# Query and key/value projections of a transformer layer as seven half-width products per pair of heads, with weights summed in place and a new first and last stretch

## Chip, core and metric

The kernel runs on one core of a Trainium2 chip. The metric is the device time of one execution in microseconds (us). The core has a matrix engine (TensorE, PE in the profile, its weight loads PEld), a vector engine (VectorE, DVE), a scalar engine (ScalarE, ACT), a general engine (GpSimd, POOL), and SyncE (SP), which here only issues DMA transfers. Each engine runs its own instruction list in order; semaphores hold an instruction until another engine has finished something.

## What is computed

A token embedding, one attention layer and one grouped feed-forward layer, for 4 sequences of 512 tokens with 1024 features, all in float32. Cut to what matters:

```python
h = table_rows(x) + edge_corrections + shards * bias + pos_emb      # (4, 512, 1024)
# attention on layernorm(h): 32 query heads, 8 key/value heads, head size 128
qkv = layernorm(h) @ w_qkv.T                                        # 4096 + 1024 + 1024 columns
scores = einsum('bskgd,btkd->bkgst', qh, kh) / sqrt(128)            # causal
attn = einsum('bkgst,btkd->bskgd', softmax(scores), vh)
h = h + attn.reshape(B, S, 4096) @ w_dense.T
# feed-forward on layernorm(h), columns permuted, 16 heads of 64, inner size 256, exact gelu
h = h + unpermute(gelu(permute(layernorm(h)) @ up) @ down)
```

## The kernel before

**Float32 products in three passes.** A float32 matrix is kept as a rounded part (`_hi`, type float32r) and a rest (`_lo`). `product` issues three matmuls for each 128x128 block of weights: hi by hi, hi by lo, lo by hi. The weights are the operand that is loaded into the array; the 512 tokens of a sequence stream through it.

**Weights.** The projections and the dense layer read tiles of 128x512 float32 (four blocks). SP loads a tile into one of the 4 buffers `w_raw`; ACT rounds it into `w_hi` (`split`, L633), POOL subtracts into `w_lo` (`low`, L927), and `w_ready` lets PE use it. `w_hi`/`w_lo` are rings of RW = 11 tiles.

**The work is a list of steps.** `schedule()` writes one list, STEPS, and every engine walks it and does its share of each step, in that order. A unit is one group g (4 query heads, one key/value head) of one sequence b; there are 32. A unit holds, for its four heads i, the steps S (scores on PE, then mask and row maximum on DVE), E (exponentials on ACT), N (division by the row sum on DVE), Ta and Tb (the probabilities turned by PE transposes into the PSUM tile `tp`), PV (probabilities times values). Between them stand projections Q (a query head), K, V of this and the next unit, eight dense steps D0 to D7 of the unit before, the feed-forward steps (P, U, O; small u and U are U steps), and at the sequence borders H, Z, Y, B, X (transposes, statistics, embedding). VT turns the value projection. The strings FIRST, MID, STATS, MLP0, MLP, GATHER, EMBED, TURN, LAST, START and REST hold the order of a unit of each sort. MID is the plain one; MLP carries one half of a pair of feed-forward blocks more. In MID the order is `S0 N0 Q2 D0 Ta0 D1 Tb0 S1 N1 Q3 D2 Ta1 D3 Tb1 S2 D4 D5 N2 D6 D7 PV0 Ta2 Q0 Tb2 S3 PV1 K N3 Q1 Ta3 PV2 Tb3 V PV3 VT`.

**A projection** (Q, K, V) is 24 matmuls of 512 columns into one of the two PSUM banks `fb` (`start_job` waits until the bank is free). ACT then copies `q_first`/`q_hi` out of the bank and DVE computes `q_lo`.

**Ta and Tb.** Ta does four transposes into the first half of `tp` and four into the second. ACT copies the first half to `pt_hi` (L655), DVE subtracts into `pt_lo` (L795), which frees it; Tb writes two more transposes into that first half and so waits on `tpa_free`, which L795 raises.

Of the kernel before, what the change touches and what calls it, by code (L numbers as in the profile page):

```python
# [59 lines left out]
MLP = ("S0 N0 Q2 q D0 Ta0 f D1 Tb0 S1 N1 Q3 D2 Ta1 D3 Tb1 S2 p F D4 D5 N2 D6 D7 u0 u1 PV0 u2 u3 Ta2 Q0 Tb2 S3 P N3 "  # L60
       "PV1 o K U0 U1 Ta3 PV2 U2 U3 Q1 Tb3 V PV3 VT")
GATHER = ("S0 N0 Q2 q A D0 Ta0 D1 Tb0 S1 N1 Q3 G0 D2 Ta1 D3 Tb1 S2 G1 D4 D5 N2 D6 G2 D7 PV0 Ta2 Q0 Tb2 S3 PV1 G3 K N3 Q1 "
          "Ta3 PV2 Tb3 V PV3 VT")
EMBED = ("S0 N0 Q2 D0 B0 Ta0 D1 B1 Tb0 S1 N1 Q3 D2 B2 Ta1 D3 B3 Tb1 S2 D4 D5 N2 D6 D7 B4 PV0 B5 Ta2 Q0 B6 Tb2 S3 B7 "
         "PV1 K N3 Q1 Ta3 PV2 Tb3 V PV3 VT")
TURN = ("S0 N0 Q2 D0 Ta0 La4 D1 Tb0 S1 N1 Lb4 Q3 Ta1 X0 D2 Tb1 X1 S2 D3 D4 N2 X2 D5 X3 D6 X4 D7 X5 PV0 X6 Ta2 X7 Tb2 S3 "
        "PV1 Q0 N3 K Q1 Ta3 PV2 Tb3 V PV3 VT")
# [69 lines left out]
JOBS = ("Q", "K", "V", "D", "H", "Z", "Y", "B", "X", "O", "end O")  # L137


class Tally:  # L140


    def __init__(self):
        jobs = [s for s in STEPS if s.kind in JOBS]
# [1 line left out]
        self.job = {s: n for n, s in enumerate(jobs)}
        self.qk = {s: n for n, s in enumerate(s for s in jobs if s.kind in ("Q", "K"))}
        self.tiles, self.tile, user = [], {}, []
        for s in jobs:
            if s.kind in ("Q", "K", "V"):  # L150
                which = {"Q": s.i, "K": HQ, "V": HQ + 1}[s.kind]
                own = [("qkv", 2 * ((HQ + 2) * s.g + which) + half) for half in range(2)]
            elif s.kind == "D":
                own = [("dense", 8 * s.g + s.i)]
            else:
                own = []
            if own:
                self.tile[s] = len(self.tiles)
            self.tiles += own
            user += [s] * len(own)  # L160


        self.user, self.splits, place = user, {s: [] for s in STEPS}, 0
        for m in range(RW):
            first = Step("X", 0, 0, min(m // 2 * 2 + 1, 7)) if m < 8 else Step("Q", 0, 0, 0)
            self.splits[first].append(m)
        for m in range(RW, len(self.tiles)):
            place = max(place, self.at[user[m - RW]])
            self.splits[STEPS[place]].append(m)
# [865 lines left out]
```

## Time and profile before

| | us |
|---|---|
| median of 3 runs | 2688.04 (2687.57 to 2689.64) |
| profiled execution, own time | 2691.08 |
| its span | 2689.3 |
| PE busy | 2603.3 (97%) |
| DVE, ACT, POOL busy | 1247.8, 1233.7, 916.6 |

The page gives the busy time of each engine, the chain of work that ended last and the costliest groups of instructions; a row of a group ends with the mean time of one instruction and with the idle time before it and who ended it. Matmuls are pipelined, so the time that one costs is read as the distance between the starts of two, in the timeline. A unit of sort MID takes 74.5 us from its first score matmul to the next unit's (364.0 to 438.5 in the timeline), one of sort MLP 83.1 us (1005.8 to 1088.9).

### The profile page before, as it was taken

The page shows a single profiled execution, that of the slowest core. Times are in us where ns is not written, and L with a number is a line of the kernel's source. Part 1 is how long each engine was busy: PE and PEld are TensorE (multiplying, and loading weights), DVE is VectorE, ACT ScalarE, POOL GpSimd, SP SyncE. Part 2 cuts the span into 40 slices and gives each one's busy share as a digit, 9 for nine tenths or more (in the row PEclk, how much of TensorE's full clock was granted, in tenths as well). Part 3 has the DMA queues.
Part 4 walks back from the last instruction along what each step waited for, and adds up shares of the span by engine and source line. Part 5 has one row for each costly group of instructions (what it writes and reads, how often), then busy time and mean ns, then how long its engine had stood idle before and what let it go on. Part 6 is the DMA issues. An engine that isn't in the chain of part 4 may idle for free.

```text
span 2689.3 us, 35616 instructions
## 1 busy us (share of the span) xinstructions
PE 2603.3 (97%) x12864; PEld 2104.8 (78%) x12864; DVE 1247.8 (46%) x3110; ACT 1233.7 (46%) x3052; POOL 916.6 (34%) x730
## 2 busy tenths in 40 slices
PE   4999999999999999999999999999999999999996
PEld 2788888887877777888887877788888778778872
DVE  4444444454544444455454444446545344434443
ACT  3544444445454454445445454544544444454432
POOL 4333333332333333433233333343332233333312
PEclk8999999999999999999999999999999999999998
DMA  4222223322322222432222222252232222222222
GB/s 126 79 67 75 75 71 109 88 75 59 102 79 82 80 75 87 125 83 63 75 87 80 86 87 78 75 137 66 69 97 72 71 87 87 91 63 75 67 75 71
DMA packets 112129, 221.49 MB, mean 82 GB/s; under 512 B 13394, under 2 KB 13394, under 8 KB 111956
## 3 DMA queue, kind: packets, MB, share of 16 engines
q1 hardware_dynamic: 104400, 193.78, 24.3%
q0 software_dynamic: 7424, 25.17, 3.4%
q8 instruction: 104, 1.70, 0.3%
q14 instruction: 69, 0.57, 0.1%
q10 hardware_dynamic: 132, 0.27, 0.0%
HBM read 202.40 MB, written 16.78 MB: 81 GB/s over the span
## 4 chain that ended last, share of the span: by engine, by line
PE 91%; DVE 4%; ACT 3%; issue 1%; DMA 0%; ACTq 0%; POOL 0%; DVEq 0%
PE fb L435 22%; PE fb L437 21%; PE fb L436 21%; PE tp L456 4%; PE sc L435 2%; PE sc L436 2%; PE sc L437 2%; PE sc L499 2%; PE fb L508 2%; PE pv L435 2%; PE pv L437 2%; PE pv L436 2%; PE sc L447 1%; ACT w_hi L633 1%; PE fb L493 1%; PE pv L468 1%
## 5 line engine op out<-in xcount | busy, mean ns | idle before, releaser
L927 POOL TENSOR_TENSOR w_lo<-w_raw,w_hi 128x512 fp32r<-128x512 f32 x640 | 818.9, 1295 | 1595.2 <-ACT w_hi L633 1595.2
L435 PE MATMUL fb<-xn_hi,w_hi 128*128 128x512 f32 x1536 | 610.8, 398 | 3.4 <-DVE stats L835 1.7
L437 PE MATMUL fb<-xn_hi,w_lo 128*128 128x512 f32 x1536 | 601.6, 392 | 0.0
L436 PE MATMUL fb<-xn_lo,w_hi 128*128 128x512 f32 x1536 | 600.4, 391 | 0.0
L633 ACT ACTIVATE w_hi<-w_raw 128x512 fp32r<-128x512 f32 x640 | 382.6, 632 | 386.7 <-PE fb L437 383.4
L435 PE MATMUL fb<-at_hi,w_hi 128*128 128x512 f32 x992 | 394.8, 398 | 8.2 <-DVE hacc L830 6.1
L649 ACT ACTIVATE prob<-sc,neg_max 128x128 f32<-128x128 f32 (+3 forms) x512 | 262.9, 526 | 280.0 <-DVE neg_max L783 279.1
L437 PE MATMUL fb<-at_hi,w_lo 128*128 128x512 f32 x992 | 387.9, 391 | 0.0
L436 PE MATMUL fb<-at_lo,w_hi 128*128 128x512 f32 x992 | 387.2, 390 | 0.0
L435 PEld LDWEIGHTS fb<-xn_hi,w_hi 128*128 128x128 f32 x1536 | 289.4, 188 | 81.8 <-issue 18.8
L437 PEld LDWEIGHTS fb<-xn_hi,w_lo 128*128 128x128 f32 x1536 | 289.2, 188 | 61.9
L830 DVE TENSOR_TENSOR hacc<-hacc,fb 128x512 f32<-128x512 f32 x256 | 175.8, 687 | 344.7 <-PE fb L437 344.1
L436 PEld LDWEIGHTS fb<-xn_lo,w_hi 128*128 128x128 f32 x1536 | 289.6, 189 | 58.4
L780 DVE CUSTOM_DVE_ANT_0 sc<-sc,mask 128x128 f32<-128x128 f32 (+3 forms) x512 | 235.6, 521 | 1.0 <-PE sc L437 0.6
L791 DVE TENSOR_SCALAR prob<-prob,inv_sum 128x128 f32<-128x128 f32 (+3 forms) x512 | 230.2, 512 | 4.5
L435 PEld LDWEIGHTS fb<-at_hi,w_hi 128*128 128x128 f32 x992 | 186.4, 188 | 58.6 <-issue 22.3
L808 DVE TENSOR_TENSOR at_lo<-pv,at_hi 128x512 fp32r<-128x512 f32 x124 | 85.4, 689 | 287.2 <-ACT at_hi L664 287.2
L437 PEld LDWEIGHTS fb<-at_hi,w_lo 128*128 128x128 f32 x992 | 186.3, 188 | 39.7
L436 PEld LDWEIGHTS fb<-at_lo,w_hi 128*128 128x128 f32 x992 | 186.6, 188 | 36.4
L813 DVE TENSOR_TENSOR q_lo<-fb,q_hi 128x384 fp32r<-128x384 f32 x128 | 71.4, 558 | 299.5 <-ACT q_hi L672 299.0
L671 ACT ACTIVATE q_first<-fb 128x128 f32<-128x128 f32 x128 | 35.4, 277 | 371.9 <-PE fb L437 371.9
L456 PEld LDWEIGHTS tp<-ident,prob 128*128 128x128 f32 x1280 | 150.8, 140 | 62.9 <-issue 18.2
(142 smaller groups left out, 3457.6 us busy)
## 6 DMA issues: line engine op xcount, KB each, us to landing
w_raw<-in_w_qkv SPq DMA_DIRECT2D x384, 256.0 KB, 2.7
w_raw<-in_w_dense SPq DMA_DIRECT2D x256, 256.0 KB, 2.6
h_rows<-hacc SPq DMA_DIRECT2D x32, 256.0 KB, 2.4
h_tok<-in_pos SPq DMA_DIRECT2D x12, 512.0 KB, 6.0
mlp_w<-in_w_mlp SPq DMA_DIRECT2D x24, 256.0 KB, 3.0
first_pos<-in_pos SPq DMA_DIRECT2D x4, 512.0 KB, 10.2
...
```

The costliest lines, as they stand in the source:

```text
L435: pe.matmul(dst, a_hi, b_hi, start=first, stop=False)
L436: pe.matmul(dst, a_hi, b_lo, start=False, stop=False)
L437: return pe.matmul(dst, a_lo, b_hi, start=False, stop=last)
L456: return pe.transpose(tp[:, at, c:c + P], prob[:, P_OFF[t] + j * P:P_OFF[t] + (j + 1) * P], ident[:, :])
L633: act.activation(w_hi[:, m % RW, :], w_raw[:, m % RAW, :], copy).then_inc(w_rounded, 1)
L649: act.activation(prob[:, P_OFF[t]:P_OFF[t] + w], sc[:, at, c:c + w], ACT.Exp, bias=neg_max[:, t:t + 1], scale=SCALE, accum_out=row_sum[:, ...
L780: dve.tensor_tensor_reduce(one, one, mask[:, S - w:S], 1.0, LOWEST, ALU.add, ALU.max, row_max[:, t:t + 1]).then_inc(tile_max, 1)
L791: dve.tensor_scalar(at, at, inv_sum[:, t:t + 1], None, ALU.mult).then_inc(prob_ready, 1)
L808: dve.tensor_tensor(lo[:, s.i, :], pv[:, :], hi[:, s.i, :], ALU.subtract).then_inc(pv_free, 1)
L813: dve.tensor_tensor(lo, fb[:, bank(s), at], hi, ALU.subtract).then_inc(bank_free[bank(s)], 1)
L830: dve.tensor_tensor(hacc[:, s.i, :], hacc[:, s.i, :], fb[:, bank(s), :], ALU.add)\
L927: pool.tensor_tensor(w_lo[:, m % RW, :], w_raw[:, m % RAW, :], w_hi[:, m % RW, :], ALU.subtract)\
```

## The change

**Seven products.** Two query heads, or the key and the value head, are projected together. The weights of the two heads form a 2x2 block matrix A (rows: heads, columns: halves of the 1024 features), the tokens a 2x2 block matrix B (rows: halves of the features, columns: halves of the 512 tokens). Instead of eight half-size products there are seven of sums and differences of blocks (the Winograd form of Strassen's scheme). A unit has three pairs: Q0 (heads 0 and 1), Q1 (heads 2 and 3), K (key and value). Each has seven tiles and seven parts of 12 matmuls with 256 columns. Q does parts 0 to 3, Qm parts 4 and 5, Qr part 6. Both banks of `fb` are used, half a bank by each part.

**Sums.** DVE forms two of the weight sums (S1, S2) in `w_raw` and POOL two (S3, S4), each 128x512. POOL does its two sums ahead of the first `low` of the pair. DVE also puts the results together out of PSUM, six instructions of 256 columns in Q and Qm and two more in Qr, and computes the `_lo` parts there. The operands B are now seven (three blocks and four sums), so there are 14 steps X per sequence in place of 8, and a new step M sums the tokens.

**Buffers.** `w_raw` is a ring of 10 in the same numbers as `w_hi`/`w_lo` (RW = 10). When a tile is loaded, summed, rounded and subtracted is set by `schedule_tiles` from a table of costs.

**Order.** All unit strings are new. Tb follows directly on Ta for most heads, K, Km, Kr stand after Tb3, and N1 and N3 stand between Qm and Qr.

**First and last stretch.** The four position sums J move from POOL to DVE, the first embedding products go through six banks, the head's order of token blocks is 0, 2, 1, 3, some activation tables are loaded early, and at the end a step `end P` runs one ahead. Several small buffers share memory.

```diff
-RAW, RW = 4, 11
+RW = 10
+HALF = S // 2
+A_USED = ("A11", "A12", "S2", "S3", "S1", "A22", "S4")
+B_USED = ("B11", "B21", "T2", "T3", "T1", "T4", "B22")
...
-MID = ("S0 N0 Q2 D0 Ta0 D1 Tb0 S1 N1 Q3 D2 Ta1 D3 Tb1 S2 D4 D5 N2 D6 D7 PV0 Ta2 Q0 Tb2 S3 PV1 K N3 Q1 Ta3 "
-       "PV2 Tb3 V PV3 VT")
+MID = ("S0 D0 N0 D1 D2 Ta0 Tb0 S1 Q1 Qm1 N1 Qr1 Ta1 Tb1 D3 S2 D4 N2 D5 D6 D7 PV0 Ta2 Tb2 S3 PV1 Q0 Qm0 N3 Qr0 Ta3 PV2 "
+       "Tb3 K Km Kr PV3 VT")
...
+                freed = self.at[self.user[(m + 5 - k if paired else m) - RW][0]]
+                wanted = start[freed] + COST[STEPS[freed].kind] + LANDING + (k * PACE if paired else 0.0)
+                n = freed + 1
+                while start[n] < wanted:
+                    n += 1
+                n = max(last, min(n, self.at[user] - 1))
+            if paired and k == 0:
+                self.sums[STEPS[n]].append(m)
+            self.splits[STEPS[n]].append(m)
...
+            def part(s, k, dst):
+                m, o = tally.tile[s] + k, OPERANDS.index(B_USED[k])
+                pe.wait_ge(w_ready, m + 1)
+                for c in range(4):
+                    w = slice(c * P, (c + 1) * P)
+                    mm = product(dst, w_hi[:, m % RW, w], w_lo[:, m % RW, w], xn_hi[:, o, c, :], xn_lo[:, o, c, :],
+                                 c == 0, c == 3)
+                mm.then_inc(prod_full, 1)
...
+                elif s.kind in ("Qm", "Km"):
+                    pe.wait_ge(out_step, 6 * pair[s] + 2)
+                    part(s, 4, fb[:, bank(s), 0:HALF])
+                    pe.wait_ge(out_step, 6 * pair[s] + 4)
+                    part(s, 5, fb[:, bank(s, 1), 0:HALF])
+                elif s.kind in ("Qr", "Kr"):
+                    pe.wait_ge(out_step, 6 * pair[s] + 6)
+                    part(s, 6, fb[:, bank(s), HALF:S])
...
+                elif s.kind in ("Qr", "Kr"):
+                    n, one, two, high = pair[s], fb[:, bank(s), :], fb[:, bank(s, 1), :], tally.high[s]
...
+                    dve.wait_ge(prod_full, 7 * n + 6)
+                    dve.tensor_tensor(other[:, 0:HALF], two[:, 0:HALF], second_out[:, 0:HALF], ALU.add)\
+                       .then_inc(bank_free[bank(s, 1)], 1)
+                    dve.wait_ge(split_hi, high + 1)
+                    dve.tensor_tensor(lo[:, own], first_out[:, own], hi[:, own], ALU.subtract)
+                    dve.wait_ge(prod_full, 7 * n + 7)
+                    dve.wait_ge(out_step, 6 * n + 6)
+                    dve.tensor_tensor(first_out[:, HALF:S], one[:, HALF:S], u2[:, :], ALU.add)\
+                       .then_inc(bank_free[bank(s)], 1)
+                    dve.wait_ge(split_hi, high + 2)
+                    dve.tensor_tensor(lo[:, HALF:S], first_out[:, HALF:S], hi[:, HALF:S], ALU.subtract)\
+                       .then_inc(first_low, 1)
+                    if s.kind == "Qr":
+                        dve.wait_ge(split_hi, high + 3)
+                        dve.tensor_tensor(q_lo[:, 1, P:S], second_out[:, P:S], q_hi[:, 1, P:S], ALU.subtract)\
+                           .then_inc(second_low, 1)
...
+            def sums_34(m):
+                n = 2 * pair[user[m][0]]
+                pool.wait_ge(w_sum12, n + 2)
+                pool.tensor_tensor(w_raw[:, (m + 3) % RW, :], w_raw[:, m % RW, :], w_raw[:, (m + 3) % RW, :],
+                                   ALU.subtract).then_inc(w_sum34, 1)
...
                 for m in splits[s]:
+                    if m in sums[s]:
+                        sums_34(m)
                     low(m)
```

**Where instructions stand, three places.** First, PE in a MID unit, from the end of the dense step that precedes Ta0 to the next score. Rows name line, instruction and the semaphores it waits for. Before:

```order
L437 MATMUL fb<-at_hi,w_lo 128x512
L456 MATMUL tp<-ident,prob 128x128 [waits tpa_free,prob_ready]
L456 MATMUL tp<-ident,prob 128x128 x3
L456 MATMUL tp<-ident,prob 128x128 [waits tpb_free]
L456 MATMUL tp<-ident,prob 128x128 x3
L435 MATMUL fb<-at_hi,w_hi 128x512 [waits bank0_free,w_ready,pv_free]
```

After:

```order
L553 MATMUL fb<-at_hi,w_lo 128x512
L572 MATMUL tp<-ident,prob 128x128 [waits tpa_free,prob_ready]
L572 MATMUL tp<-ident,prob 128x128 x3
L572 MATMUL tp<-ident,prob 128x128 [waits tpb_free]
L572 MATMUL tp<-ident,prob 128x128 x3
L572 MATMUL tp<-ident,prob 128x128 [waits tpa_free]
L572 MATMUL tp<-ident,prob 128x128
L563 MATMUL sc<-k_first,q_first 128x128 [waits exp_done,g_done,second_low,first_low]
```

The dense step that stood between Ta and Tb has moved ahead of Ta; Tb's wait on `tpa_free` now comes right behind Ta. Second, DVE in a MID unit, from N3 to the sums for K. Before:

```order
L791 TENSOR_SCALAR prob<-prob,inv_sum 128x512
L813 TENSOR_TENSOR q_lo<-fb,q_hi 128x384 [waits split_hi]
L795 TENSOR_TENSOR pt_lo<-tp,pt_hi 128x512 [waits tpa_hi]
L798 TENSOR_TENSOR pt_lo<-tp,pt_hi 128x384 [waits tpb_hi]
```

After:

```order
L951 TENSOR_SCALAR prob<-prob,inv_sum 128x512
L994 TENSOR_TENSOR second_out<-fb,second_out 128x256 [waits prod_full]
L997 TENSOR_TENSOR q_lo<-first_out,q_hi 128x128 [waits split_hi]
L1000 TENSOR_TENSOR first_out<-fb,u 128x256 [waits out_step,prod_full]
L1003 TENSOR_TENSOR q_lo<-first_out,q_hi 128x256 [waits split_hi]
L1007 TENSOR_TENSOR q_lo<-second_out,q_hi 128x384 [waits split_hi]
L955 TENSOR_TENSOR pt_lo<-tp,pt_hi 128x512 [waits tpa_hi]
L958 TENSOR_TENSOR pt_lo<-tp,pt_hi 128x384 [waits tpb_hi]
L1141 TENSOR_TENSOR w_raw<-w_raw 128x512 [waits w_in9,w_in1,prod_full,job_full]
L1145 TENSOR_TENSOR w_raw<-w_raw 128x512 [waits w_sum12,w_in6]
```

Five instructions of Qr now stand ahead of `pt_lo` where one stood, and the two sums for K's weights behind it. Third, POOL at the same place; before it has only `low` there, after:

```order
L1160 TENSOR_TENSOR w_raw<-w_raw 128x512 [waits w_sum12]
L1165 TENSOR_TENSOR w_raw<-w_raw 128x512 [waits w_in7,prod_full]
L1171 TENSOR_TENSOR w_lo<-w_raw,w_hi 128x512 [waits w_rounded,w_sum34]
L1171 TENSOR_TENSOR w_lo<-w_raw,w_hi 128x512 [waits w_rounded] x9
```

POOL's own two sums now stand between DVE's sums and the first `w_lo` of K.

## Rows read from the trace of the kernel before

**Rows 1.** The page: busy time (share) and instructions of each engine; the chain.

```profile
PE 2603.3 (97%) x12864; PEld 2104.8 (78%) x12864; DVE 1247.8 (46%) x3110; ACT 1233.7 (46%) x3052; POOL 916.6 (34%) x730
PE 91%; DVE 4%; ACT 3%; issue 1%; DMA 0%; ACTq 0%; POOL 0%; DVEq 0%
```

**Rows 2.** Waits of PE from 80 to 2590 us: total, times, longest.

```profile
PE tp L456 <- DVE pt_lo L795: 9.3, 22, 1.5
```

**Rows 3.** Timeline of PE: start, duration, instruction; 512 columns, then 256.

```profile
667.67 0.39 PE L436 MATMUL fb<-xn_lo,w_hi 128*128 128x512 f32 x1
...
669.48 0.39 PE L435 MATMUL pv<-pt_hi,v_hi 128*128 128x512 f32 x1
...
670.69 0.29 PE L435 MATMUL pv<-pt_hi,v_hi 128*128 128x256 f32 x1
...
671.06 0.38 PE L468 MATMUL pv<-pt_last,v_last 128*128 128x128 f32 x2
671.28 0.60 PE L539 MATMUL tp<-ident,prob 128*128 128x128 f32 x4
671.71 0.39 PE L447 MATMUL sc<-k_first,q_first 128*128 128x128 f32 x2
```

**Rows 4.** Timeline: a Ta, and the ACT and DVE work that frees it.

```profile
448.48 1.04 PE L456 MATMUL tp<-ident,prob 128*128 128x128 f32 x8
449.21 0.58 ACT L655 ACTIVATE pt_hi<-tp 128x512 fp32r<-128x512 f32 x1
449.83 0.69 DVE L795 TENSOR_TENSOR pt_lo<-tp,pt_hi 128x512 fp32r<-128x512 f32 x1 [0.46 <-ACT pt_hi L655]
```

**Rows 5.** Timeline of PE: a Ta with only four transposes before Tb.

```profile
638.14 1.04 PE L456 MATMUL tp<-ident,prob 128*128 128x128 f32 x8
639.02 0.60 PE L493 MATMUL fb<-ident,row_buf 128*128 128x128 f32 x4
640.32 0.44 PE L456 MATMUL tp<-ident,prob 128*128 128x128 f32 x2 [0.70 <-DVE pt_lo L795]
```

**Rows 6.** Timeline: normalisation N on DVE, and POOL with three tiles.

```profile
444.32 0.18 DVE L787 RECIPROCAL inv_sum<-row_sum 128x4 f32<-128x4 f32 x1 [2.21 <-ACT prob L649]
444.54 1.27 DVE L791 TENSOR_SCALAR prob<-prob,inv_sum 128x128 f32<-128x128 f32 x4
447.20 3.79 POOL L927 TENSOR_TENSOR w_lo<-w_raw,w_hi 128x512 fp32r<-128x512 f32 x3 [7.03 <-ACT w_hi L633]
```

**Rows 7.** Groups by shape, 80 to 2590 us: busy, mean ns of one, idle before.

```profile
L803 DVE TENSOR_TENSOR pt_lo<-tp,pt_hi 128x256 fp32r<-128x256 f32 x127 | 53.3, 420 | 42.6 <-ACT pt_hi L661 42.6
L791 DVE TENSOR_SCALAR prob<-prob,inv_sum 128x128 f32<-128x128 f32 x127 | 80.3, 632 | 4.5
L813 DVE TENSOR_TENSOR q_lo<-fb,q_hi 128x384 fp32r<-128x384 f32 x126 | 70.3, 558 | 289.4 <-ACT q_hi L672 289.0
L661 ACT ACTIVATE pt_hi<-tp 128x256 fp32r<-128x256 f32 x127 | 47.6, 375 | 4.2 <-PE tp L456 4.0
L672 ACT ACTIVATE q_hi<-fb 128x384 fp32r<-128x384 f32 x126 | 61.3, 487 | 0.0
L898 DVE TENSOR_TENSOR y<-y,rstd 128x512 f32<-128x512 f32 x24 | 16.6, 692 | 0.8
L499 PE MATMUL sc<-y,mlp_w 64*128 64x512 f32 x192 | 55.1, 641 | 0.0
L726 ACT ACTIVATE g<-sc 128x512 f32<-128x512 f32 x96 | 52.9, 613 | 2.3 <-PE sc L499 0.5
L726 ACT ACT_TABLE_LOAD x24 | 30.8, 1283 | 5.4 <-PE sc L499 5.1
```

**Rows 8.** Stretches near the end: length, busy time by engine, granted clock (column PEclk), DMA.

```profile
60.90:2631.10 2570.20, 2539.53 (x12663) 2079.28 (x12661) 1201.15 (x3033) 1193.07 (x2982) 874.48 (x694) 1.00 0.28 81
2631.20:2641.30 10.10, 6.81 (x12) 2.78 (x14) 4.43 (x14) 3.63 (x6) 6.52 (x7) 0.50 0.67 198
```

**Rows 9.** Timeline of PE: the first work after the clock had fallen.

```profile
2632.26 2.08 PE L574 MATMUL fb<-y,ones 128*128 128x512 f32 x2 [2.50 <-DVE y L846]
```

More of the change, by code:

```diff
@@ L60 @@
[L60 to L67, printed above, removed]
@@ new lines @@
+STATS = ("S0 D0 N0 D1 D2 Ta0 Tb0 S1 Q1 Qm1 N1 Qr1 Ta1 Tb1 D3 S2 D4 N2 D5 D6 D7 PV0 Z0 Z1 Ta2 Z2 Z3 Tb2 S3 Z4 Z5 PV1 Q0 "
+         "Qm0 N3 Qr0 Z6 Ta3 PV2 Z7 Tb3 K Km Kr PV3 VT")
+MLP0 = ("S0 Y0 Y1 H0 N0 H1 H2 H3 D0 Ta0 Tb0 S1 Q1 Qm1 N1 Qr1 Ta1 H4 H5 Tb1 S2 H6 D1 H7 f D2 N2 D3 D4 D5 p F D6 D7 u0 "
+        "u1 PV0 u2 u3 Ta2 Tb2 S3 P PV1 o Q0 Qm0 N3 Qr0 U0 U1 Ta3 PV2 U2 U3 Tb3 K Km Kr PV3 VT")
+MLP = ("S0 q D0 N0 f D1 D2 Ta0 Tb0 S1 Q1 Qm1 N1 Qr1 Ta1 Tb1 D3 S2 p F D4 N2 D5 D6 D7 u0 u1 PV0 u2 u3 Ta2 Tb2 S3 P PV1 o Q0 "
+       "Qm0 N3 Qr0 U0 U1 Ta3 PV2 U2 U3 Tb3 K Km Kr PV3 VT")
@@ new lines @@
+GATHER = ("S0 q D0 N0 D1 D2 Ta0 Tb0 S1 Q1 Qm1 N1 A Qr1 Ta1 Tb1 D3 S2 D4 N2 G0 D5 D6 G1 D7 PV0 Ta2 Tb2 S3 G2 PV1 Q0 Qm0 N3 G3 "
+          "Qr0 Ta3 PV2 Tb3 K Km Kr PV3 VT")
+EMBED = ("S0 B0 D0 N0 B1 D1 D2 Ta0 B2 Tb0 S1 Q1 Qm1 N1 Qr1 Ta1 B3 Tb1 D3 S2 D4 N2 D5 D6 D7 B4 PV0 B5 Ta2 Tb2 B6 S3 B7 PV1 "
+         "Q0 Qm0 N3 Qr0 Ta3 PV2 Tb3 K Km Kr PV3 VT")
+TURN = ("S0 La4 D0 N0 Lb4 D1 D2 Ta0 Tb0 S1 Q1 Qm1 N1 Qr1 Ta1 X0 X1 M0 Tb1 S2 X2 D3 X3 D4 N2 X4 D5 X5 D6 X6 D7 PV0 X7 X8 M1 "
+        "Ta2 Tb2 S3 X9 X10 PV1 X11 X12 X13 Q0 Qm0 N3 Qr0 Ta3 PV2 Tb3 K Km Kr PV3 VT")
@@ L75, in unit @@
+LANDING, PACE = 3.5, 1.4
 def unit(order, b, g):
@@ L136 @@
 STEPS = schedule()
-JOBS = ("Q", "K", "V", "D", "H", "Z", "Y", "B", "X", "O", "end O")
+JOBS = ("D", "H", "Z", "Y", "B", "X", "O", "end O")
+PARTS = {"Q": ("Q", "Qm", "Qr"), "K": ("K", "Km", "Kr")}
+PART_OF = (0, 0, 0, 0, 1, 1, 2)
 class Tally:
     def __init__(self):
-        jobs = [s for s in STEPS if s.kind in JOBS]
         self.at = {s: n for n, s in enumerate(STEPS)}
[L146 to L169, printed above, removed]
@@ L176, in __init__, with schedule_tiles @@
         self.la = {s: n for n, s in enumerate(s for s in STEPS if s.kind == "La")}
+    def schedule_tiles(self):
+        start, now = [], 0.0
+        for s in STEPS:
+            start.append(now)
+            now += COST.get(s.kind, 0.0)
+        self.loads, self.sums, self.splits = ({s: [] for s in STEPS} for _ in range(3))
+        n, last = 0, 0
+        for m, (name, _) in enumerate(self.tiles):
+            user, k = self.user[m]
+            paired = user.kind not in JOBS
+            if name != "sum" and m >= RW:
+                self.loads[self.user[m - RW][0]].append(m)
+            if m < len(A_USED):
+                n = self.at[Step("X", 0, 0, 3)] + m
+            else:
+                freed = self.at[self.user[(m + 5 - k if paired else m) - RW][0]]
[7 more added lines that the diff above has]
+            self.splits[STEPS[n]].append(m)
+            last = n
 def tower_kernel(nc, x_cols, x_row, table, bias, pos, edge_cols, w_qkv, w_dense, w_mlp, perm_cols, out):
@@ L573, in _ @@
                     dst = start_job(s)
[L574 removed]
+                    pe.matmul(dst, ones[:, :], root_wide if s.i else mean_wide, start=True, stop=True)\
                         .then_inc(job_full, 1)
```

477 lines of the change are left out of this document (309 added, 168 removed).

## The prediction, made before the changed kernel ran

> **What bounds the kernel now.** I read the page first: PE is busy for 2603.3 of 2689.3 us and is 91% of the chain that ended last [rows 1]. The waits of PE come next: from 80 to 2590 us its largest is 9.3 us in all, for `pt_lo`, the half of `tp` that Tb writes [rows 2]. So PE's own list sets the time, and the other engines have slack only because PE finds something else to do while they work. Two questions follow: what the new list costs PE by itself, and whether PE still finds something to do.
>
> **Products: a gain of 75 us.** In the timeline eight starts of 512-column matmuls lie 1.81 us apart together, 0.226 each; three of 256 columns lie 0.37 apart, 0.123 each [rows 3]. Half the columns cost more than half the time. A pair had 2 x 24 matmuls, 10.9 us; it now has 7 x 12, 10.1 us at 0.120, a value between 0.123 and half of 0.226. Over 96 pairs: 4608 x 0.2264 = 1043 us before, 8064 x 0.120 = 968 us after. Ends: 8064 x 0.113 = 911 (gain 132) and x 0.127 = 1024 (gain 19); I take 75, near the row that shows 256 columns.
>
> The Trainium skill ("TensorE: Matmul & The Clock Gate", section "Back-to-back issue gap") puts an isolated matmul at its columns over 2.4 GHz plus 2.5 ns, so 216 and 109 ns. The rows show 226 and 123 [rows 3]. By the page the gain would be an estimated 96 x (48 x 0.216 - 84 x 0.109) = 116 us.
>
> **More operand transposes: 11 us.** Six more X steps in each of 4 sequences, four transposes each, 96 x 0.11 (four from 671.28 to 671.71) [rows 3].
>
> **Tb right behind Ta.** Ta's eight transposes start at 448.48; ACT's copy runs to 449.79, DVE's `pt_lo` to 450.52 [rows 4]: 2.04 us from Ta to the release. The eight take 0.87 us, so a Tb with nothing ahead of it waits 1.2 us. A row shows this: with 0.4 us of transposes between, Tb still waited 0.70 and started 2.18 us after Ta [rows 5]. Before, a dense or projection step of 2.7 us or more stood there. The order listing puts Tb right behind Ta for heads 0 to 2 of nearly every unit. Three prices:
> Tb0: 1.2 us, 29 units (EMBED has a small job between): 35 us.
> Tb2: PV0's copy and subtraction stand ahead on ACT and DVE, so 1.35 us, 16 units: 22 us. In the 12 units with feed-forward (MLP, MLP0) four gelus of 0.61 and a table load of 1.28 stand ahead on ACT [rows 7], of which PE covers PV0 (1.8 us, 669.48 to 671.28) and four U steps at 0.29 (55.1 us over 192) [rows 3, 7]: about 2.4 us, 29 us in all.
> Tb1 waits for DVE's work of Qr, next.
>
> **DVE's chain behind Qm and Qr.** Count from the end of part 4. DVE sees it at 0.2, does two adds of 256 columns (0.42, overlapping) [rows 7] until 0.9, then N: 1.49 us from 444.32 to 445.81 [rows 6], to 2.4. Part 6 ends at 2.9 (two parts of 12 x 0.12). The last add ends at 3.5, ACT's copy (0.375) at 3.9, DVE's `_lo` (0.42) at 4.35, ACT's copies for the second head (0.26 by the slope of the rows, and 0.487) at 4.5, DVE's `q_lo` (0.558) at 5.1 [rows 7]. Only then come ACT's `pt_hi` (to 5.0) and DVE's `pt_lo` (to 5.7). PE had finished Ta1 at 3.75: Tb1 waits 2.0 us, in 25 units 50 us. N can be longer while POOL works: its instruction of 128 columns averages 632 ns, where four instructions took 1.27 us in the row [rows 6, 7]; that is the high end, 1 us more each.
> Ta3 has PV2 (1.8 us) between itself and Tb3, which covers nearly all.
>
> **K's weights.** Behind `pt_lo` (5.7) DVE does the second `pt_lo` (to 6.2) and K's sums S1 and S2, 0.69 each [rows 7]: 7.5. POOL follows with S3, S4 and the first `low`, three at 1.26 (3.79 for three) [rows 6]: 11.35. PE has done Qr, Ta3, PV2, Tb3 by 5.9. So K waits 5.5 us, 5.65 with Tb3's rest. After that POOL's 1.26 a tile keeps ahead of PE's 1.44 a part. 19 units: 107 us. In the 12 units with feed-forward the sums stand ahead of Ta3's `pt_lo` (K ready at 10.3) and PE has 1.1 us of U steps more: 3.45 us, 41 us. The wait that bounds K is thus DVE, then POOL; the page's busy shares hide it, for neither engine is full.
>
> **Borders, head and tail: 34 us.** FIRST and MLP0 put H and Y right behind S, but ACT copies them only after E, which ends at 444.3 in a unit that starts at 438.5 [rows 6]: some 4.7 and 3 x 4 us. TURN's last X steps run through two banks: 3 x 4. Head: DVE gets J and twice the X work, K there waits too: +10. Tail: table loads and an earlier `end P`: -5.
>
> **The clock.** TensorE was granted 2.4 GHz (1.00) from 60.9 to 2631.1 us, with no wait over 1.5 us of that kind, then 1.2 GHz (0.50) for 10.1 us [rows 2, 8]. Ahead of the fall PE did nothing from 2629.8 on, 1.4 us [rows 9]. The wait for K, 5.5 us, is longer than that. A fall loses half of its length where PE has work: 5 us at most by this row, about 3 where the wait itself takes part of it. At 3 us in most of the 19 units, and a few elsewhere: 50 us.
>
> The Trainium skill (the same page, section "What's actually happening") says that the slow clock is the default and that activity releases it; the trace agrees, full speed through the whole dense stretch and half in the gaps near the end. By it the long waits cost twice, in themselves and in the work behind them.
>
> **The sum.** Gain -75. Transposes +11. Waits Tb 35 + 22 + 29 + 50 = 136; K 107 + 41 = 148; borders 34; clock 50. Together +304. The profiled execution took 2691.1 us (its span plus 1.8), 3 above the median: 2688 + 304 = 2992. I say 2990.
>
> **Rivals.**
> (a) The same waits, no fall of the clock: 2940. For it: PE fills the waits with little but does have Tb3 in them. Against: the fall at 2631.
> (b) Other side, faster. The mechanism is PE's cadence at 256 columns together with engines that run ahead: if DVE reached K's sums about 5.6 us earlier, as the cost table of the change assumes (the sums right after Qr, not behind N3, Qr and Ta3 on DVE), K would wait nothing and the clock would hold. Then only Tb's waits remain at their floor, 82 x 1.2 = 98, and the borders 10 to 34. With the gain at 75 that is 2688 - 75 + 11 + 98 + 20 = 2742; with the gain at its end of 132, 2685. It becomes faster from the point where all waits of a unit fall below 2 us (64 us over 32 units). Against it: rows 4 and 5 give 1.2 us for each of three Tb a unit, 3.6 us. Faster means 2620 to 2680.
> (c) K's weights in time, Tb's waits as I have them: 2688 - 75 + 11 + 136 + 34 = 2794.
> (d) The change doesn't do what it says: the order listing shows 84 matmuls of 256 columns a pair, so I give it nothing.
> (e) Worse: N stretched by POOL each time (+1 us x 56) and a fall of the clock in every unit at both long waits (+80): 3128.
>
> **Chances.** Forecast with falls 0.45, (a) 0.22, (c) and the space between it and (a) 0.16, (e) 0.09, (b) 0.08, of which faster by over 0.2% is 0.05 and within it 0.02 (0.2% is about what a measurement of this kernel can tell from no change). Slower: 0.93. The range runs from 2830, which leaves out (c) and (b), to 3090.
>
> **What would show it.** Right: PE's waits list `tp` behind DVE `pt_lo` some 80 times or more, near 130 us in all, and the first product of K behind POOL `w_lo` 31 times, near 150; a MID unit takes 82 to 86 us in place of 74.5, an MLP unit near 90; starts at 256 columns lie 0.117 to 0.127 apart; the granted clock is below 1.00 between 80 and 2590. Wrong: PE still over 95% busy, K starting less than 2 us behind Tb3, or Tb starting under 1.5 us behind Ta. Then the chain on DVE is shorter than its instructions' durations add up to, and the gain of the products decides.

## The result, and the profile after

The changed kernel took 3128.18 us (median of 4 runs, 3124.47 to 3132.30), the kernel before 2688.84 us (2687.57 to 2690.00) beside it: a ratio of 1.163, 95% interval 1.1616 to 1.1653. That is slower, as forecast, but 439 us slower where the sum said 304, and outside the range.

The page of the changed kernel, its busy times and its chain, to be held against [rows 1]:

```profile
PE 2669.4 (85%) x16416; PEld 2312.4 (74%) x16416; DVE 1826.6 (58%) x4228; ACT 1389.1 (44%) x3430; POOL 1504.9 (48%) x1206
PE 45%; issue 23%; DVE 13%; POOL 10%; ACT 9%; DMA 0%; ACTq 0%; DVEq 0%; POOLq 0%
```

PE carried 91% of the chain before and carries 45% now. The time is in PE's waits. From 80 to 3020 us (total, times, longest), where [rows 2] had 9.3 us at the top:

```profile
PE tp L572 <- DVE pt_lo L955: 175.8, 106, 5.5
PE fb L551 <- POOL w_lo L1171: 120.8, 32, 7.6
PE fb L619 <- DVE xn_lo L1085: 23.8, 9, 5.5
PE fb L619 <- ACT high_tok L846: 14.2, 3, 4.7
PE tp L572 <- DVE prob L951: 14.1, 14, 5.3
PE fb L619 <- ACT hacc L841: 12.9, 5, 5.6
```

One MID unit, 358.0 to 443.4 us, shows where they are; these are the first instruction of Tb0, Tb1, Tb2 and of K in PE's timeline, with the idle time before each in brackets, and the two matmuls behind the last (to be held against [rows 3 to 5]):

```profile
370.92 0.44 PE L572 MATMUL tp<-ident,prob 128*128 128x128 f32 x2 [0.98 <-DVE pt_lo L955]
...
386.01 0.44 PE L572 MATMUL tp<-ident,prob 128*128 128x128 f32 x2 [1.91 <-DVE pt_lo L955]
...
406.63 0.44 PE L572 MATMUL tp<-ident,prob 128*128 128x128 f32 x2 [2.06 <-DVE pt_lo L955]
...
429.40 0.55 PE L551 MATMUL fb<-xn_hi,w_hi 128*128 128x256 f32 x1 [5.43 <-POOL w_lo L1171]
429.75 0.41 PE L552 MATMUL fb<-xn_lo,w_hi 128*128 128x256 f32 x1
429.96 0.41 PE L553 MATMUL fb<-xn_hi,w_lo 128*128 128x256 f32 x1
```

The prediction had 1.2, 2.0, 1.35 and 5.5 us. After the long wait the starts are 0.21 us apart, at the low clock (granted 0.50); elsewhere the median of over 7500 starts at 256 columns is 0.120 us. Next come four kinds of stretches (length, busy time of PE, PEld, DVE, ACT, POOL, granted clock, DMA share, GB/s): the head, FIRST, a MID unit, a TURN unit.

```profile
0.00:104.00 104.00, 54.98 (x253) 40.45 (x253) 46.98 (x90) 30.24 (x58) 27.99 (x28) 0.77 0.25 81
104.00:187.40 83.40, 62.41 (x417) 58.29 (x418) 42.94 (x114) 38.58 (x99) 37.89 (x30) 0.86 0.15 42
358.00:443.40 85.40, 74.22 (x483) 67.89 (x482) 48.70 (x120) 36.52 (x98) 44.26 (x35) 0.96 0.22 62
706.10:822.10 116.00, 87.92 (x539) 78.60 (x538) 64.27 (x145) 51.30 (x119) 44.13 (x35) 0.90 0.16 46
```

In the kernel before the same four, from score to score, were 80.9, 59.7, 74.5 and 82.4 us long. MID grew by 10.8 us, as forecast (82 to 86 us), an MLP unit from 83.1 to 92.4; but TURN grew by 33.6, FIRST by 23.7 and the head by 23.1, and those I had at 10 to 20 us each. Only the stretch from LAST to the end got shorter, from 144.2 to 138.1 us.

### The profile page after: what moved, and what is told of

It reads as the page before. It is cut to its first block, busy times and chain, and to the rows that moved or that the text cites. A ratio compares the mean times of both kernels' runs of the same rounds, so it can differ in the third digit from the quotient of the medians.

```text
span 3127.8 us, 45082 instructions
## 1 busy us (share of the span) xinstructions
PE 2669.4 (85%) x16416; PEld 2312.4 (74%) x16416; DVE 1826.6 (58%) x4228; ACT 1389.1 (44%) x3430; POOL 1504.9 (48%) x1206
## 4 chain that ended last, share of the span: by engine, by line
PE 45%; issue 23%; DVE 13%; POOL 10%; ACT 9%; DMA 0%; ACTq 0%; DVEq 0%; POOLq 0%
PE fb L551 11%; PE fb L552 11%; PE fb L553 11%; POOL w_lo L1171 7%; DVE prob L951 3%; ACT prob L796 2%; DVE sc L940 2%; POOL w_raw L1165 2%; PE tp L572 1%; DVE neg_max L943 1%; DVE pt_lo L955 1%; PE sc L552 1%; PE sc L551 1%; PE sc L553 1%; ACT w_hi L783 1%
## 5 line engine op out<-in xcount | busy, mean ns | idle before, releaser
L1171 POOL TENSOR_TENSOR w_lo<-w_raw,w_hi 128x512 fp32r<-128x512 f32 x928 | 1176.9, 1311 | 324.7 <-ACT w_hi L783 316.6
L551 PE MATMUL fb<-xn_hi,w_hi 128*128 128x256 f32 x2688 | 789.8, 294 | 139.5 <-POOL w_lo L1171 120.8
L552 PE MATMUL fb<-xn_lo,w_hi 128*128 128x256 f32 x2688 | 778.6, 290 | 0.0
L553 PE MATMUL fb<-xn_hi,w_lo 128*128 128x256 f32 x2688 | 777.4, 289 | 0.0
L1160 POOL TENSOR_TENSOR w_raw<-w_raw 128x512 f32<-128x512 f32 x96 | 124.1, 1293 | 1112.2 <-DVE w_raw L1145 1112.2
L551 PEld LDWEIGHTS fb<-xn_hi,w_hi 128*128 128x128 f32 x2688 | 535.5, 199 | 162.8 <-issue 137.2
L783 ACT ACTIVATE w_hi<-w_raw 128x512 fp32r<-128x512 f32 x928 | 540.4, 638 | 129.0 <-DVE w_raw L1145 93.2
L552 PEld LDWEIGHTS fb<-xn_lo,w_hi 128*128 128x128 f32 x2688 | 535.6, 199 | 1.6
L553 PEld LDWEIGHTS fb<-xn_hi,w_lo 128*128 128x128 f32 x2688 | 533.7, 199 | 0.0
L572 PE MATMUL tp<-ident,prob 128*128 128x128 f32 x1280 | 193.9, 283 | 193.9 <-DVE pt_lo L955 178.0
```

The source lines that it names most:

```text
L551: pe.matmul(dst, a_hi, b_hi, start=first, stop=False)
L552: pe.matmul(dst, a_hi, b_lo, start=False, stop=False)
L553: return pe.matmul(dst, a_lo, b_hi, start=False, stop=last)
L572: return pe.transpose(tp[:, at, c:c + P], prob[:, P_OFF[t] + j * P:P_OFF[t] + (j + 1) * P], ident[:, :])
L783: act.activation(w_hi[:, m % RW, :], w_raw[:, m % RW, :], copy).then_inc(w_rounded, 1)
L1160: pool.tensor_tensor(w_raw[:, (m + 3) % RW, :], w_raw[:, m % RW, :], w_raw[:, (m + 3) % RW, :], ALU.subtract).then_inc(w_sum34, 1)
```

## The experiments

All are the kernel before or the changed kernel with one thing edited. Ratios are to the kernel before, on the same chip, with 95% intervals.

### The price of a Tb that stands right behind its Ta: e4, e1

e4 gives the kernel before, with its old products, nothing but the new neighbourhood:

```
-MID = "S0 N0 Q2 D0 Ta0 D1 Tb0 S1 N1 Q3 D2 Ta1 D3 Tb1 S2 D4 D5 N2 D6 D7 PV0 Ta2 Q0 Tb2 S3 ...
+MID = "S0 N0 Q2 D0 D1 Ta0 Tb0 S1 N1 Q3 D2 D3 Ta1 Tb1 S2 D4 D5 N2 D6 D7 PV0 Q0 Ta2 Tb2 S3 ...
```

The strings of the other kinds of units are changed in the same way.

> The kernel before, with its own products of 512 columns, and with one thing of the changed one: each of Ta0 Tb0, Ta1 Tb1 and Ta2 Tb2 stands together, what stood between moved ahead of Ta. Theory (a Tb that stands right behind its Ta costs 1 to 2 us, whatever the projections are): 3 x 1.0 to 2.0 us in 31 units, 140 us, and some falls of the clock, 20 us: 2850 us (2800 to 2880). Waits of tp for pt_lo rise from 9 to about 140 us. Rival (the waits are the price of the new scheme's load on VectorE, not of the order): 2690 to 2740 us.

Measured: 2875.39 us, ratio 1.069 (1.0673 to 1.0709). The waits for `pt_lo`, from 80 to 2780 us:

```profile
PE tp L456 <- DVE pt_lo L795: 141.1, 112, 2.2
```

The theory holds: +186 us, of which 132 are these waits, with the old products and a DVE that is hardly busier than before (1259.8 us for 1247.8). Of the other 54 us some 17 are the clock (it was low for 57 us, 18 before) and 14 are PE's other waits. So this one habit of the new order costs more than twice what the seven products save.

e1 is the reverse, in the changed kernel:

```
-MID = "S0 D0 N0 D1 D2 Ta0 Tb0 S1 Q1 Qm1 N1 Qr1 Ta1 Tb1 D3 S2 D4 N2 D5 ...
+MID = "S0 D0 N0 D1 D2 Ta0 D3 Tb0 S1 Q1 Qm1 N1 Qr1 Ta1 D4 Tb1 S2 D5 N2 D6 ...
```

> The changed kernel with other order strings and nothing else: in every kind of unit but TURN and LAST a product of the output weights (a D step, 24 matmuls, 2.7 us) stands between Ta0 and Tb0, and another between Ta1 and Tb1; FIRST has an H step between Ta0 and Tb0, and Tb2 stays as it is. Theory (each Tb that stands right behind its Ta waits for one copy and one subtraction, and a step between them hides it): the two waits of a plain unit, 0.98 and 1.91 us, go, about 2.9 us x 25 units = 72 us, and some of the clock's falls go with them: 3045 us (3030 to 3065). Waits of tp for pt_lo fall from 176 to about 90 us. Rival (the wait is VectorE's queue, and whatever stands there is late as well): the waits move to other places, 3110 to 3130 us.

(A D step is 12 matmuls of 512 columns, 2.7 us, not 24.) Measured: 3067.37 us, ratio 1.141 (1.1391 to 1.1429), 61 us less than the changed kernel and 2 above the range. A MID unit fell from 85.3 to 82.2 us. From 80 to 2960 us:

```profile
PE fb L551 <- POOL w_lo L1171: 120.8, 32, 7.6
PE tp L572 <- DVE pt_lo L955: 91.1, 53, 5.5
PE tp L572 <- DVE prob L951: 32.1, 25, 6.8
```

85 us of waits for `pt_lo` went and 18 us for `prob` came. The four multiplications of N2 (summed over the 32 of them) had gone from 41.8 to 140.2 us of DVE. The new order had brought POOL's splits beside them: POOL was at work in 1 of the 41.8 us, and in 124 of the 140.2. That was not in any theory; the next runs show what it is.

### K's weights, and what stands beside GpSimd: e2, e9, e10

```
-                wanted = start[freed] + COST[STEPS[freed].kind] + LANDING + (k * PACE if paired else 0.0)
+                landing = 0.0 if user.kind in PARTS["K"] and STEPS[freed + 1].kind == "Qm" else LANDING
+                wanted = start[freed] + COST[STEPS[freed].kind] + landing + (k * PACE if paired else 0.0)
```

> The changed kernel with one number of its planner changed: the sums and splits of K's weights are put in the queues as soon as the first four products of Q0 are over (right behind Qm0), not 3.5 us later. Theory (K's first product waits since its weights are summed too late, not since GpSimd can't keep up): the 31 waits of fb for w_lo, 121 us in all (5.43 us in a plain unit), fall to under 1 us each; the sums stand ahead of N3 on VectorE now and make Ta3 up to 0.7 us later, 20 us in all; in plain units the clock's one fall (6.8 us long) comes in that wait and goes with it, 3 us each. 3000 us (2970 to 3030). Rival (GpSimd's two sums and seven splits at 1.25 us, 11.3 us of work for 10 us of products, are the bound): the wait is spread over the seven products, 3090 to 3125 us.

Measured: 3185.97 us, ratio 1.184 (1.1823 to 1.1862): 58 us slower than the changed kernel, where 128 us less was expected. K's waits did go (from 120.8 to 3.5 us), but the waits for `prob` came (from 14.1 to 142.7). The rows show N3 on DVE, the first transposes of Ta3 on PE behind it, and what POOL did meanwhile:

```profile
417.59 5.42 DVE L952 TENSOR_SCALAR prob<-prob,inv_sum 128x128 f32<-128x128 f32 x4
...
423.06 1.97 PE L573 MATMUL tp<-ident,prob 128*128 128x128 f32 x8 [4.91 <-DVE prob L952]
...
417.55 1.28 POOL L1161 TENSOR_TENSOR w_raw<-w_raw 128x512 f32<-128x512 f32 x1 [11.42 <-DVE w_raw L1146]
418.79 1.26 POOL L1166 TENSOR_TENSOR w_raw<-w_raw 128x512 f32<-128x512 f32 x1
420.13 4.01 POOL L1172 TENSOR_TENSOR w_lo<-w_raw,w_hi 128x512 fp32r<-128x512 f32 x3
```

The four multiplications that take 1.27 us in [rows 6] took 5.42, about as long as four operations of POOL that ran at the same time; so it was in all 32 units (170.2 us together, and POOL at work throughout). e9 puts the sums behind N3 and changes nothing else: `landing` is 2.7 in the place of 0.0.

> As e2_early, but K's sums stand behind N3 on VectorE and not ahead of it (1.4 us later, still 1.8 us earlier than in the changed kernel). In e2 the four multiplications of N3 took 5.42 us instead of 1.27 while GpSimd ran its sums of K's weights, and Ta3 waited 4.9 us for them. Theory (VectorE's multiplications by a column, from SBUF to SBUF, don't get on beside a running GpSimd operation, and nothing else was wrong with e2): N3 takes 1.3 us again, Ta3's wait goes, K's 31 waits fall from 121 us to under 20, and the time to 3128 - 105 - 15 = 3008 us (2985 to 3030). Rival (the earlier sums themselves, in whatever place, hold up the chain of Q0's outputs): 3100 to 3190 us.

Measured: 3107.91 us, ratio 1.156 (1.1536 to 1.1575). The same unit, N3, the next two subtractions of the Q outputs on DVE, and Tb3 on PE:

```profile
416.86 1.28 DVE L952 TENSOR_SCALAR prob<-prob,inv_sum 128x128 f32<-128x128 f32 x4
...
419.79 1.27 DVE L998 TENSOR_TENSOR q_lo<-first_out,q_hi 128x128 fp32r<-128x128 f32 x1
...
422.48 1.52 DVE L1008 TENSOR_TENSOR q_lo<-second_out,q_hi 128x384 fp32r<-128x384 f32 x1
423.93 0.68 DVE L956 TENSOR_TENSOR pt_lo<-tp,pt_hi 128x512 fp32r<-128x512 f32 x1
...
424.66 0.69 PE L573 MATMUL tp<-ident,prob 128*128 128x128 f32 x2 [3.16 <-DVE pt_lo L956]
```

N3 is at 1.28 us again, and the 78 us against e2 are the placing alone: the theory that VectorE's multiplications are held up beside GpSimd holds. The number did not. K's waits fell from 120.8 to 9.3 us, yet the kernel won 20 us and not 120. Now the subtractions whose two operands lie in SBUF run beside POOL, 1.27 and 1.52 us for what took 0.28 and 0.56 in the changed kernel (the `pt_lo` behind them, whose one operand is read from PSUM, keeps its 0.68). They stand ahead of `pt_lo`, Tb3 waits 3.16 us where it waited nothing, and the clock falls there (423.8 to 430.6 us) and once more early in the unit (382.8 to 386.2), with PE's work in most of it and not K's wait. A MID unit took 85.3 us as in the changed kernel; the 20 us came from other units. The waits for `pt_lo` went from 175.8 to 230.8 us between 80 and 3020 us. A wait was taken off PE, and its cause left on DVE.

e10 keeps e2's place and moves the multiplications to ACT:

```
-                        dve.tensor_scalar(at, at, inv_sum[:, t:t + 1], None, ALU.mult).then_inc(prob_ready, 1)
+                        act.activation(at, at, copy, scale=inv_sum[:, t:t + 1]).then_inc(prob_ready, 1)
```

> e2_early with the four multiplications of every N step on ScalarE (a copy with a scale) instead of VectorE; the weights' sums stand where e2 has them, beside N3. Theory (only VectorE's multiplications are held up by GpSimd): N takes about 2.1 us everywhere, as the exponentials of the same shapes do, in the 32 places N3 where e2 needs 5.4 and in the 32 places N0 where the changed kernel needs 4.05; Ta3's waits for prob fall from 137 us to under 25 and the time from 3186 to about 3060 us (3020 to 3090). Rival (whichever engine reads and writes SBUF beside GpSimd is held up, ScalarE too): N3 stays above 4 us and the time above 3150 us.

Measured: 3143.33 us, ratio 1.169 (1.1667 to 1.1720). All 512 multiplications, in one group of the page's kind:

```profile
L804 ACT ACTIVATE prob<-prob,inv_sum 128x128 f32<-128x128 f32 (+3 forms) x512 | 246.1, 553 | 374.1 <-DVE inv_sum L953 374.1
```

1.92 us for each N, beside POOL or not (the 32 N3 stand beside POOL throughout, the 32 N1 hardly ever, and both take 1.92 to 1.93 us): ACT is not held up, DVE is. The mechanism is the theory's; the gain, 43 us, is a third of what was expected, again because Tb waited instead (219.5 us for `pt_lo`). The Trainium skill ("SBUF — State Buffer", section "SBUF: two separate sides") says that VectorE and GpSimd share one pair of ports as an exclusive lock, taken by a VectorE operation in a 2-port mode or, against a GpSimd operation that reads SBUF, with two SBUF inputs, and that ScalarE never waits. By that rule `q_lo<-first_out` (two SBUF inputs, 1.27 us for 0.28) is held up, `pt_lo<-tp` (0.68) and N on ScalarE (1.92) are not: the rows agree. N on VectorE (5.42 us for 1.28) has one SBUF input and fits the rule if it runs in a 2-port mode, which no run here shows by itself.

### The clock: e3

```
+            def keep(dst, n):
+                for _ in range(n):
+                    pe.matmul(dst, k_hi[:, 0:P], k_hi[:, 0:HALF], start=True, stop=True)
...
+                        keep(sc[:, 2, 0:HALF], (8, 14, 16)[s.i])
...
+                        keep(one[:, 0:HALF], 24 if s.b > 0 and 0 < s.g < 6 else 38)
```

> The changed kernel with matmuls added whose results are overwritten: TensorE does 8, 14 or 16 products of 256 columns (0.96, 1.7, 1.9 us) while it would wait between Ta0 and Tb0, Ta1 and Tb1, Ta2 and Tb2 (not the last in units that have U steps), and 38 (4.6 us; 24 in units with U steps) ahead of K's first product. They fit into the waits, so that no wait gets shorter and nothing else starts earlier. Theory (the clock falls because TensorE is idle in these waits, and it costs about 90 us in all, on top of the waits): low clock between 60 us and the end falls from 318 to under 100 us, and the time to about 3065 us (3040 to 3090). Rival (the clock goes by something else than these waits, or what it costs is hidden in the waits): 3120 to 3150 us, the added matmuls being at best neutral.

Measured: 3115.13 us, ratio 1.159 (1.1569 to 1.1608). From 60 us to the end the clock was low for 159 us in place of 316, and the time fell by 13 us, where 63 were forecast. A MID unit with the fillers, and at full clock throughout:

```profile
354.20:438.00 83.80, 81.70 (x559) 75.48 (x558) 49.14 (x120) 36.47 (x98) 44.54 (x35) 1.00 0.22 64
```

Two things lie in the gap. First, a fall costs less than half its length: in the MID unit it lasted 6.8 us, 426.1 to 432.9, 3.3 of them inside K's wait, and taking it away brought 1.5 us. Second, in STATS and MLP0 the fillers are longer than the waits (K waits 1.4 us in a unit with U steps, and I gave it 24 matmuls), and these units got 1 to 5 us longer. Over the whole kernel the 1954 fillers take some 234 us (at 0.120), while the waits fell by 196 and what is lost at their ends (below) by 8, so the fillers themselves cost about 30 us. Counted from starts (each start in a low stretch against the median of its shape at full clock, 0.213 against 0.120 at 256 columns, 0.427 against 0.227 at 512, 0.213 against 0.109 at 128), the low clock costs, over the whole span, 112 us in the changed kernel, 61 in e3 and 12 in the kernel before. So 13 us are what the run shows net of its own cost; the 51 us between 112 and 61 are a count over rows, and they fit the run with the 30 set against them (21, with 18 measured between the profiled spans).

### The products: e5

```
-                    for half in range(2):
+                    for cols in (slice(0, S // 2), slice(S // 2, S)):
+                        for half in range(2):
...
+                                mm = product(dst[:, cols], w_hi[:, m % RW, w], w_lo[:, m % RW, w],
+                                             xn_hi[:, 4 * half + k, cols], xn_lo[:, 4 * half + k, cols],
```

> The kernel before with each of its 4608 projection matmuls of 512 columns made two of 256 (the same sums, 9216 matmuls), everything else as it was. Theory (256 columns cost 0.120 us from start to start, over half of the 0.2264 us of 512): 9216 x 0.120 - 4608 x 0.2264 = +63 us, 2752 us (2735 to 2765). With it seven products in place of eight save 75 us on the matmuls, not 130. Rival (the shorter matmul costs half, and the time is lost elsewhere): 2690 to 2705 us.

Measured: 2741.71 us against 2688.14, +54 us, ratio 1.020 (1.0184 to 1.0218). It lies in the range and the theory holds: (1043 + 54) / 9216 = 0.119 us a matmul of 256 columns, and seven products save 1043 - 8064 x 0.119 = 83 us, near the 75 of the sum.

### TURN: e6

```
-        "... Qr1 Ta1 X0 X1 M0 Tb1 S2 X2 D3 X3 D4 N2 X4 D5 X5 D6 X6 D7 PV0 X7 X8 M1 Ta2 Tb2 S3 X9 X10 PV1 ..."
+        "... Qr1 Ta1 X0 Tb1 X1 S2 D3 M0 X2 D4 N2 X3 X4 D5 X5 X6 D6 X7 X8 D7 PV0 Ta2 M1 Tb2 X9 S3 X10 PV1 ..."
```

> The changed kernel with another order in the three TURN units and nothing else: the sums M0 (four on VectorE, 2.8 us) move from between X1 and Tb1 to behind S2 and D3, M1 from ahead of Ta2 to behind it, and the X steps are spread over the D steps. Theory (TURN is 116 us, 34 more than before, because M0 and X0, X1 stand ahead of S2's maxima and M1 ahead of Tb2 on VectorE): 10 to 16 us less in each TURN, 3128 - 40 = 3088 us (3075 to 3100). Rival (fourteen transposes with two banks and eight sums bound the unit however they stand): 3115 to 3130 us, TURN at 112 us or more.

Measured: 3119.27 us, ratio 1.161 (1.1590 to 1.1628), TURN 112 us in the place of 116: 4 us each, not 10 to 16, and the rival is nearer. In the changed kernel four waits of a TURN are long: Tb0 (4.7 us), the step X2 (5.5), Tb2 (5.4) and K (5.4). PE's list from 706.1 to 822.1 us:

```profile
PE tp L572 <- DVE pt_lo L955: 11.2, 3, 5.4
PE fb L619 <- DVE xn_lo L1085: 7.9, 3, 5.5
PE fb L551 <- POOL w_lo L1171: 5.4, 1, 5.4
PE fb L551 <- DVE xn_lo L1085: 1.4, 1, 1.4
```

M1 ahead of `pt_lo` is the 5.4 us of Tb2: with M1 moved, Tb2 waits 1.5. X2's wait went too, but a later X step waits 4.1 us for a free bank. Tb0 still waits 4.7 us in e6, for its cause was not moved: the layer norm of the next sequence's tokens (`La`, `Lb`) now stands ahead of Ta0, and its ACT work ahead of `pt_hi`:

```profile
718.09 1.24 ACT L787 ACTIVATE row_buf<-h_tok,shift,rstd 128x1024 f32<-128x1024 f32 x1 [3.07 <-DVE shift L1079]
719.24 1.23 ACT L787 ACTIVATE high_tok<-h_tok,shift,rstd 128x1024 f32<-128x1024 f32 x1
...
721.41 0.57 ACT L802 ACTIVATE pt_hi<-tp 128x512 fp32r<-128x512 f32 x1
...
722.76 0.69 PE L572 MATMUL tp<-ident,prob 128*128 128x128 f32 x2 [4.71 <-DVE pt_lo L955]
```

No run tried `Lb` in another place. Fourteen X steps and eight sums had no place that cost nothing in the two orders tried; which order would be the best one was not searched for.

### Everything together, and one step too far: e7, e8, e11

e7 takes e1's order and also moves Q0 between Ta2 and Tb2 (`... PV0 Ta2 Q0 Tb2 S3 PV1 Qm0 N3 Qr0 Ta3 ...`); both have e2's line in the planner, which in this order acts in TURN and the head alone, since elsewhere Q0 is no longer followed by Qm0. e8 differs from e7 by e6's TURN and nothing else.

> The order of e1_cover, and in every unit but TURN and LAST the first four products of Q0 (5.8 us) moved between Ta2 and Tb2 as well, so that every Tb of these units has cover, and S3 and PV1 (3.7 us) lie between Q0 and Qm0, which gives K's weights that much more time. Theory (waits and falls of the clock are the loss): against the changed kernel the waits of Tb, 2.9 + 2.1 us in 28 units, and 3.7 of the 5.4 us of K's go, 75 + 55 + 100, and most falls of the clock outside TURN, 50 to 70 us: 2850 us (2820 to 2900). Rival (GpSimd or VectorE is near its limit and gives the wait elsewhere): 2950 to 3000 us.

> The order of e7_third, the TURN of e6_turn, and in TURN and LAST's neighbour the earlier place of K's sums of e2_early. Theory (they add): e7's 2850 less 40 us for TURN and 20 us for its K wait and clock: 2790 us (2750 to 2850), still slower than before, by what the head (+23), FIRST (+24) and TURN (+15 each) keep. Rival (with all waits gone the 75 us of the matmuls come through): under 2690 us.

Measured: 3122.23 us (1.162, 1.1600 to 1.1638) and 3104.84 us (1.155, 1.1519 to 1.1583). Both miss by about 300 us (272 and 315). PE's list of e7 from 80 to 3000 us names the reason:

```profile
PE tp L573 <- DVE prob L952: 134.7, 53, 6.8
PE fb L552 <- DVE second_out L983: 57.6, 28, 2.7
PE tp L573 <- DVE pt_lo L956: 50.3, 24, 5.4
```

Tb has its cover, and N3 now stands beside POOL's sums as in e2 (its 32 sum up to 170 us of DVE for 42), while Qm's sums on DVE stand behind S3's maxima. e11 puts together only what had helped so far: e1's order, e9's place, e10's N, e6's TURN.

> All that helped at once: the order of e1_cover, K's sums behind N3 as in e9, N on ScalarE as in e10, the TURN of e6. Theory (the waits were most of the loss, and nothing in the scheme forbids hiding them but the head, FIRST and TURN): a plain unit at 76 to 77 us (85.3 in the changed kernel, 74.5 before), a unit with U steps at 84 to 86, TURN at 105, head and FIRST as in the changed kernel: 2870 us (2840 to 2910), still 5 to 8% over the kernel before. Rival (ScalarE or VectorE becomes the bound once N is on ScalarE): over 2950 us.

Measured: 2964.49 us, ratio 1.102 (1.0997 to 1.1034): 164 us less than the changed kernel, though 94 over the expected time and in the rival's range. The rival's mechanism is not shown: ACT and DVE are each busy for 55% of the span. The unit that was forecast at 76 to 77 us:

```profile
338.50:414.80 76.30, 72.63 (x483) 66.41 (x482) 43.87 (x104) 43.53 (x114) 44.42 (x35) 1.00 0.25 70
659.30:769.10 109.80, 89.17 (x539) 79.13 (x538) 56.24 (x129) 57.94 (x135) 44.12 (x35) 0.91 0.18 51
```

The MID unit in the first row has 3.6 us of waits left; taken off, they leave 72.7 us, under the 74.5 of before. By this subtraction, and by e5, the gain of the products is there; no run shows a unit in which PE waits for nothing, and none that is shorter than before. Head 102.5, FIRST 82.2, TURN 109.8 (second row), MLP0 102 and MLP 87 to 88 us keep the kernel at 2964, and the summed waits for `pt_lo` are still 122.7 us.

### The tail alone, in the kernel before: e12

```
-    for p in range(PAIRS):
-        steps += end("P", p) + end("U", 4 * p) + end("U", 4 * p + 1)
+    steps += end("P", 0)
+    for p in range(PAIRS):
+        if p + 1 < PAIRS:
+            steps += end("P", p + 1)
+        steps += end("U", 4 * p) + end("U", 4 * p + 1)
...
+                    if s.b == B - 1:
+                        act.activation(warm[:, 1:2], ones[:, 0:1], ACT.Gelu)
```

> The kernel before, projections and all, with the changed kernel's tail and nothing else of it: VectorE centres and scales the rows of pair p + 1 before TensorE's products of pair p (the step end P one place earlier), the first of them no longer waits for the second broadcast, and the ScalarE table of the last stage is loaded before it is needed. Theory (the tail is a change of its own, and it is worth the difference of the rounds, 3.8 us against 5.1, that the changed kernel's trace shows there, times 7, and 1 us at its start): 2689 - 10 = 2679 us (2676 to 2683). Rival (the shorter rounds of the changed kernel hang on something else of it): 2687 to 2690 us.

Measured: 2679.61 us against 2689.49, ratio 0.9968 (0.9956 to 0.9980): inside the expected range, and the one run that is faster than the kernel before. In the chain that ended last, before, DVE's add (L911) and the two steps of `end_y` (L905, L907) lay between the rounds of the last stage, which were 5.1 us apart; now they are 3.8 apart. Before, then e12:

```profile
2642.63 1.89 PE fb L508 x8
2644.55 0.69 DVE h_tok L911
...
2645.87 0.70 DVE end_y L907
...
2647.75 1.89 PE fb L508 x8
```

```profile
2638.92 1.87 PE fb L512 x8
...
2642.70 1.87 PE fb L512 x8
...
2646.49 1.87 PE fb L512 x8
```

## Why the prediction was right in kind and wrong in size

PE's waits over the whole span rose from 74.1 to 445.1 us, +371. With the products and transposes (-75 + 11), the clock by count of starts (112 against 12, +100) and the ends of the waits (+28, last item) that makes 435 of the 438.5 by which the profiled span grew. By the steps of the sum:

- **Products, -75: right.** e5 gives 0.119 us at 256 columns.
- **Waits of Tb, 136: measured +169** (178.0 less 9.3). Tb0 (0.98 for 1.2) and Tb1 (1.91 for 2.0) were right, and so was the reason, as e4 and e1 show. Mis-sized were Tb2 in a MID unit (2.06 for 1.35) and the three TURN units, whose waits are 11.2 us each (`Lb` on ACT ahead of `pt_hi`, M1 on DVE ahead of `pt_lo`) where the sum had at most about 4.5.
- **K's weights, 148: measured 121.** 5.43 us in a MID unit (5.5), but 1.4 and not 3.45 in a unit with U steps.
- **Borders, head and tail, 34: measured +81, one of the two steps that failed most.** That is what all other waits grew by, from 64.8 to 146.3 us. The H steps behind S were near the forecast (5.6 us for 4.7 in FIRST, 4.7 for 4 in MLP0). What was missed is the rest of DVE's and ACT's queues: in the head, which grew by 23.1 us and not by 10 (K waits 7.6 us there), in FIRST (a Ta waits 5.3 us for `prob`) and in TURN (X steps wait 7.9 us for a bank and not 4).
- **The clock, 50: +100 by count, the other one.** The price of a fall was not too low (3 us; e3 gives 1.5 for the one of a MID unit, and 100 us over 61 more falls are 1.6 each), their number was: I had one in most of the 19 units with the long wait for K and a few elsewhere, and there were 64 after 60 us, against 3 before, four in each TURN and one or two in the units with U steps, where K waits 1.4 us. Beside the counted 100, e3 shows 13 us net for half of the low time.
- **Not in the sum: the ends of the waits, 28 us.** A wait is counted from the end of the last matmul, and that lies later than the start that could have followed: a matmul of 256 columns lasts 0.29 us, while starts are 0.12 apart [rows 3]. By the starts this is 0.2 us for each wait, 45 us over 232 waits in the changed kernel and 17 over 77 before. In e4 it is 33 us, 16 more than before, of the 54 that its waits for `pt_lo` did not explain. The ends of matmuls are modelled in the profile, so the border between a wait and its end is only as good as that; the sum of the two is not touched by it.

Rival (e) gave 3128, the very time, and that is luck: it had N stretched in 56 places for 56 us on PE, while in the changed kernel it is stretched in the 32 places N0 (4.05 us, mostly hidden by D steps), and PE waits 14 us for it. Its falls, about two a unit for 130 us, were nearer to the 64 counted than mine. Rival (c) had K's weights in time at 2794 us; e9 did that and got 3108: the step that failed in it is the thought that a wait taken from PE leaves nothing behind. Rival (a), no falls, is refuted by the 64 falls. Rival (b) wanted all waits of a unit under 2 us, and no run got there: e11 comes nearest, with 3.6 us in a MID unit, which is still 1.8 us over before.
